# Full-height contraction for the product that adds the row maxima in an attention kernel

## The chip, the cores and the metric

The kernel runs on one core of one Trainium2 chip. The metric is device time in microseconds (us) of one launch, from the runs shown below. TensorE (PE in the profile, PEld for its weight loads) multiplies, VectorE (DVE), ScalarE (ACT) and GpSimd (POOL) do the elementwise work, and SyncE (SP) issues most DMAs. Every engine takes its own instructions in their written order and waits on semaphores.

## What is computed

The input x is 16 batches of 512 tokens of 256 channels, in float32. Four layers follow one another, each on a layer norm of x and added back to x: a gated delta net (a recurrence over the tokens, 16 heads), a mixture of experts (16 experts, 4 chosen for a token, and one shared), causal softmax attention (16 heads of 16 channels, with RMS norm and rotary embedding of queries and keys), and the mixture again. Only the third layer is touched by the change:

```
attn = einsum('bhqd,bhkd->bhqk', q, k) / sqrt(16)
attn = softmax(attn + causal, axis=-1)        # causal: -inf above the diagonal
out  = einsum('bhqk,bhkd->bhqd', attn, v) @ Wo
```

A softmax needs the largest score of each query subtracted ahead of the exponential. The kernel does it on TensorE, while the scores are still being summed in PSUM.

## The kernel before

The first half of the span (up to about 2970 us) is the recurrence, a chain of small VectorE steps, with the first mixture beside it. The second half is attention and the second mixture of all 16 batches. `stages()` writes out one list of named stages in Python, by generators that are stepped in turn with rates and costs; each engine then goes through this list and emits its own part of each stage. So the order on every engine is fixed, and interleaves the attention of a batch b, the end of the first mixture (batches 12 to 15, during the attention of batch 0), and the second mixture of earlier batches.

Attention of a batch: project (b_qk, b_v), normalize and rotate, split queries and keys into bfloat16 parts (s_...), turn them (s_turn), so that qT and kT hold 128 rows for each head (8 parts of 16 channels). Then come four groups of four heads. For a group, `largest(hg)` writes the scores with the queries on the partitions (m_dot, lines 1009 and 1011) and VectorE takes their row maxima, negated (m_max, L1367). The maxima are split into three bfloat16 parts (m_part), turned (m_turn, L1020) and copied by ScalarE into the tile mT: 12 rows (3 parts of 4 heads) by 512 queries (m_out, L1686). There are two mT tiles, one in the tile `region` and one in `w_attn`, which the profile names so.

`weigh(hg)` then makes the scores again, with the keys on the partitions, 16 times for a group (4 blocks of 128 keys by 4 heads; the width is 512, 384, 256 or 128 queries). This is w_dot, and it has three products into one PSUM bank: the scores (L1028, 128 rows of contraction), the negated maxima (L1030, 12 rows: a column of the selection matrix sel4 repeated over 128 columns, against the 12 rows of mT), and the causal mask on the diagonal block (L1032, 128 rows, 128 columns). ScalarE takes the exponential (w_exp, L1692) into one of eight buffers P, and w_pv (L1045) multiplies by the values, four heads side by side in 32 columns each. There are 16 x 4 x 16 = 1024 w_dots and 1024 m_dots. `largest(hg)` and `weigh(hg - 1)` are stepped in turn, so m_dot and w_dot alternate for three of the four weigh groups, and the last weigh group of a batch runs without m_dots.

PSUM banks come from the list `misc`: three banks until the first mixture is done, seven after that. m_max or w_exp gives the bank back.

In the second mixture, the tokens of a group of two or four batches are scattered to the rows of their experts in DRAM: x_row (ScalarE, L1721) makes a tile of 128 tokens and x_move (GpSimd, L1847) sends it with four indirect DMAs, for 8 or 16 tiles in a row. ScalarE waits in x_row until the move of two tiles before has landed.

GpSimd prepares the constants of attention once, in second_setup (L1820 to L1830): it counts the semaphore bset up to 7, and the engines that use a constant wait for its number. The lines around the change:

Of the kernel before, what the change touches and what calls it, by code (L numbers as in the profile page):

```python
# [9 lines left out]
BF = mybir.dt.bfloat16  # L10
# [4 lines left out]
NB, SEQ, D, H, HD = 16, 512, 256, 16, 16  # L15
# [703 lines left out]
def build(nc, T, out):  # L719
# [6 lines left out]
    psum = nc.alloc_psum_tensor("psum", [128, 8, 512], FP)  # L726
# [44 lines left out]
    def inshared(at, shape):  # L771
        return within(shared[:, at:at + math.prod(shape)], shape)
# [16 lines left out]
    lowerE, thr, tcol, upper32 = (inshared(2112, [NE, NE]), inshared(2368, [NE]), inshared(2384, [1]),  # L789
                                  inshared(2400, [128]))  # L790
    upper, onesb = shared[:, 2528:2592].bitcast(BF), shared[:, 2592:2656].bitcast(BF)
    sel4, sel432 = shared[0:12, 2916:2918].bitcast(BF), inshared(2920, [4])
    cosT, sinT = inshared(2924, [NQ, HD]), inshared(2988, [NQ, HD])
    qT, kT = partb(0, [16, 512]), partb(4096, [16, 512])
    vb = part(8192, [NQ, 16, 32])
# [55 lines left out]
    s = Sems(nc)  # L851
# [15 lines left out]
    def tensor():  # L867
# [4 lines left out]
        for name, *u in order:  # L872
# [149 lines left out]
            elif name == "w_dot":  # L1022
# [4 lines left out]
                pe.wait_ge(s[mf[0]], mf[1])  # L1027
                e.matmul(psum[:, mi, 0:n], kT[:, h, keys], qT[:, h, kt * 128:SEQ], start=True, stop=False,  # L1028
                         skip_group_check=True)
                e.matmul(psum[:, mi, 0:n], sel4[:, a:a + 1].broadcast_to([12, 128]), mT[k % 2][0:12, kt * 128:SEQ],  # L1030
                         start=False, stop=False, skip_group_check=True)
                o = e.matmul(psum[:, mi, 0:128], maskb[:, :], identb[:, :], start=False, stop=True,  # L1032
                             skip_group_check=True)
# [494 lines left out]
    def scalar():  # L1528
        ac = Eng(nc.scalar)
        e = nc.scalar  # L1530
        for name, *u in order:
# [98 lines left out]
            elif name == "f_up":  # L1630
                h, c, x, xi, xt, ti, gi, gf, si, sf = u
                ac.wait_ge(s["fup"], 34 * h + 17 * c + x + 1)
                ac.wait_ge(s[sf[0]], sf[1])
                if h >= 12:
                    o = e.activation(sil[si][:, :], psum[:, gi, 0:256], ACT.Tanh, scale=0.5)
                else:
                    o = e.activation(sil[si][:, :], psum[:, gi, 0:256], ACT.Silu)  # L1637
                o.then_inc(s["fs"], 1)
            elif name == "second_setup":
                ac.wait_ge(s["oadd"], 64)  # L1640

            elif name == "b_qk_out":
                i, mi, ai, af = u
                ac.wait_ge(s["qkm"], i + 1)
                ac.wait_ge(s["lo"], max(i - 3, 0))
                e.activation(qkr[i % 4], bank_of(mi), ACT.Copy).then_inc(s["qkc"], 1)
                ac.wait_ge(s[af[0]], af[1])
                e.activation(ra[ai], bank_of(mi), ACT.Square).then_inc(s["qks"], 1)
            elif name == "b_v_out":
                i, mi, ai = u  # L1650
                ac.wait_ge(s["vm"], i + 1)
                ac.wait_ge(s["pv"], 64 * (i // 4))
                ac.wait_ge(s["bset"], 7)
                e.activation(vb[:, i % 4, :, 0:16], psum[:, mi, 0:D].rearrange("p (h e) -> p h e", e=16),
                             ACT.Copy).then_inc(s["ve"], 1)
            elif name == "b_rms":
                b, = u
                ac.wait_ge(s["rm1"], b + 1)
                e.activation(rm, rm, ACT.Sqrt).then_inc(s["rm2"], 1)
            elif name == "s_hi":  # L1660
                i, ci, cf = u
                hh, cm = heads(qkr[i % 4]), comb3[ci]
                ac.wait_ge(s["spr"], 4 * i + 4)
                ac.wait_ge(s[cf[0]], cf[1])
                ac.wait_ge(s["pv"], 64 * (i // 4))
                e.activation(cm[:, 0:16, 0:3, :], bc(hh[:, 0:16, :], 2, 3), ACT.Copy)
                e.activation(cm[:, 16:32, 0:8:3, :], bc(hh[:, 16:32, :], 2, 3), ACT.Copy).then_inc(s["sph"], 1)
            elif name == "s_mid":
                i, ci = u
                hh, cm = heads(qkr[i % 4]), comb3[ci]  # L1670
                ac.wait_ge(s["r1"], 2 * i + 1)
                e.activation(cm[:, 16:32, 1:8:3, :], bc(hh[:, 16:32, :], 2, 3), ACT.Copy).then_inc(s["ma"], 1)
            elif name == "s_out":
                i, n, t, mi = u
                if n % 2:
                    j = slice(i % 4 * 128, i % 4 * 128 + 128)
                    ac.wait_ge(s["spt"], t)
                    ac.wait_ge(s["pv"], 64 * (i // 4))
                    e.activation((qT if n < 2 else kT)[:, 8:16, j],
                                 bank_of(mi).bitcast(BF).rearrange("p (h t) -> p h t", h=8),  # L1680
                                 ACT.Copy).then_inc(s["eva"], 1)
            elif name == "m_out":
                k, mi = u
                ac.wait_ge(s["pt"], k + 1)
                ac.wait_ge(s["ws"], 16 * max(k - 1, 0))
                e.activation(mT[k % 2][0:12, :], bank_of(mi).bitcast(BF)[0:12, 0:512], ACT.Copy).then_inc(s["mt"], 1)  # L1686
            elif name == "w_exp":
                k, kt, a, mi = u
                w, n = 16 * k + 4 * kt + a, SEQ - kt * 128
                ac.wait_ge(s["ws"], w + 1)  # L1690
                ac.wait_ge(s["pv"], max(w - 7, 0))
                e.activation(P[w % 8][:, 0:n], psum[:, mi, 0:n], ACT.Exp, scale=HD ** -0.5).then_inc(s["we"], 1)  # L1692
            elif name == "w_out":
                k, = u
                ac.wait_ge(s["pv"], 16 * k + 16)
                ac.wait_ge(s["pr"], k // 4 * 4)
                e.activation(oT[:, k % 4, :], psum[:, 6, :], ACT.Copy).then_inc(s["otr"], 1)
            elif name == "c_copy":
                i, mi, ci, cf = u
                ac.wait_ge(s["pt2"], i + 1)  # L1700
                ac.wait_ge(s[cf[0]], cf[1])
                e.activation(otc[ci][:, :, :], psum[:, mi, 0:256].rearrange("p (k t) -> p k t", k=2),
                             ACT.Copy).then_inc(s["poc"], 1)

            elif name == "g_score":
                b, mi, rf = u
                ac.wait_ge(s["glg"], b + 1)
                ac.wait_ge(s[rf[0]], rf[1])
                e.activation(r_sc, logits(bank_of(mi)), ACT.Tanh, scale=0.5).then_inc(s["gth"], 1)
            elif name == "g_act":  # L1710
                z, mi, si, sf = u
                ac.wait_ge(s["gu"], z + 1)
                ac.wait_ge(s[sf[0]], sf[1])
                e.activation(sil[si][:, :], psum[:, mi, 0:256], ACT.Tanh, scale=0.5).then_inc(s["gs"], 1)
            elif name == "x_row":
                g, J = u
                b, j = J // 4, J - ROWS0[g]
                ac.wait_ge(s["rv"], RV0[g] + 15 + 4 * GROUPS[g])
                if J >= 2:
                    ac.wait_ge(s[f"move{J % 2}"], 64 * (J // 2))  # L1720
                e.activation(srow[J % 2], x1[(b + 4) % 5][:, J % 4, :], ACT.Identity, bias=stq[:, j, 1:2],  # L1721
                             scale=stq[:, j, 0:1]).then_inc(s["row"], 1)
            elif name == "t_turned":
                I, mi = u
                ac.wait_ge(s["xT"], I + 1)
                ac.wait_ge(s["f1"], max(I - 1, 0))
                e.activation(xgT[I % 2], psum[:, mi, 0:256].rearrange("p (k t) -> p k t", k=2),  # L1727
                             ACT.Copy).then_inc(s["xe"], 1)
            elif name == "t_gate":
                I, mi, si, sf, hi, hf = u  # L1730
                ac.wait_ge(s["f1"], I + 1)
                ac.wait_ge(s[sf[0]], sf[1])
                e.activation(sil[si][:, 0:128], psum[:, mi, 0:128], ACT.Tanh, scale=0.5).then_inc(s["t1"], 1)  # L1733
            elif name == "t_hturned":
                I, mi = u
                ac.wait_ge(s["th"], I + 1)
                ac.wait_ge(s["f2"], max(I - 1, 0))
                e.activation(hT[I % 2], psum[:, mi, 0:128], ACT.Copy).then_inc(s["he"], 1)
            elif name == "t_out":
                g, I, mi = u  # L1740
                ac.wait_ge(s["f2"], I + 1)
                ac.wait_ge(s[f"yr{I % 2}"], 16 * (I // 2))
                e.activation(yrow[I % 2], psum[:, mi, 0:D], ACT.Copy).then_inc(s["yo"], 1)

    def gpsimd():
        po = Eng(nc.gpsimd)
        e = nc.gpsimd
        for name, *u in order:
# [71 lines left out]
            elif name == "second_setup":  # L1820
                po.wait_ge(s["oadd"], 64)
                po.wait_ge(s["d_b"], 176)
                e.tensor_copy(upper, upper32).then_inc(s["bset"], 1)
                e.tensor_copy(sel4, sel432[0:12, :]).then_inc(s["bset"], 1)
                e.memset(onesb, 1.0).then_inc(s["bset"], 1)
                e.tensor_tensor(cw, bc(cosT[:, :, :], 2, 2), bc(nw, 1, NQ), ALU.mult).then_inc(s["bset"], 1)
                e.tensor_tensor(sw, bc(sinT[:, :, :], 2, 2), bc(nws, 1, NQ), ALU.mult).then_inc(s["bset"], 1)
                e.memset(vb, 0.0).then_inc(s["bset"], 1)
                po.wait_ge(s["bset"], 6)
                e.memset(vb[:, :, :, 16:17], 1.0).then_inc(s["bset"], 1)  # L1830
            elif name == "g_score":
                b, mi, rf = u
                po.wait_ge(s[rf[0]], rf[1])
# [182 lines left out]
```

## Time and profile before

| | us |
|---|---|
| median of 3 runs | 5931.54 (5925.28 to 5931.58) |
| the profiled execution | 5932.07 |
| its span, first to last instruction | 5930.8 |
| PE busy | 4571.4 (77%) |
| DVE busy | 4165.5 (70%) |
| ACT busy | 1978.3 (33%) |
| POOL busy | 873.5 (15%) |
| mean granted TensorE clock | 0.883 of full speed |

"Busy" is an average over stages with different limits, so the table does not say what bounds the kernel. Matmuls overlap in the engine: the duration of one in the profile includes its way through the array, and what one costs on a busy TensorE is the distance from its start to the start of the next one. The chain of waits follows the execution back from its last instruction, and gives each engine and line the time for which it alone held up the end.

### The profile page before, as it was taken

Reading aid. Unit: us, or ns where it says so; the run is one execution under the profiler, and the core shown is the slowest. Engines: PE = TensorE matmul, PEld = TensorE weight load, DVE = VectorE, ACT = ScalarE, POOL = GpSimd, SP = SyncE. Lnnn points to the kernel's source line nnn. Section 1 sums busy time; section 2 is a strip of 40 time slices with the busy share of each in tenths; the row PEclk is TensorE's granted clock in tenths of the full one; section 3 lists DMA queues with packets and bytes.
Section 4 is the critical chain, followed back from the end, with each engine's and each line's share of the span. In section 5 each row is a group of like instructions: output and inputs, shape, how many; then the busy total and the mean of one; then the engine's idle time right before and its main releaser. Section 6 shows DMA issues by size and latency. Waiting matters only on the chain.

```text
span 5930.8 us, 70668 instructions
## 1 busy us (share of the span) xinstructions
PE 4571.4 (77%) x23962; PEld 3026.4 (51%) x23962; DVE 4165.5 (70%) x9356; ACT 1978.3 (33%) x4665; POOL 873.5 (15%) x1157
## 2 busy tenths in 40 slices
PE   6321188977988768877899879977999788978875
PEld 3110155655656556656667545543555455555553
DVE  1999999999999999994544555564555566555523
ACT  3111022212222121101322455553556455545442
POOL 2011011101010010001000020024000422023434
PEclk8655589998999989998999989987999799988987
DMA  1210000000000000000000011112111222122445
GB/s 73 112 41 5 2 10 11 11 4 15 10 12 4 9 6 8 8 4 27 11 4 8 8 44 43 44 56 71 43 45 48 85 76 86 46 74 71 140 149 155
DMA packets 192498, 249.28 MB, mean 42 GB/s; under 512 B 25744, under 2 KB 169744, under 8 KB 191888
## 3 DMA queue, kind: packets, MB, share of 16 engines
q1 hardware_dynamic: 167568, 177.63, 9.3%
q0 software_dynamic: 24576, 67.14, 3.6%
q8 instruction: 196, 3.21, 0.2%
q14 instruction: 158, 1.29, 0.1%
HBM read 120.94 MB, written 123.73 MB: 41 GB/s over the span
## 4 chain that ended last, share of the span: by engine, by line
PE 44%; DVE 36%; issue 9%; POOL 4%; ACT 4%; DMA 2%; SPq 0%; DVEq 0%; ACTq 0%; POOLq 0%
PE psum L956 7%; DVE rec L1200 4%; DVE rec L1213 4%; DVE rec L1202 4%; DVE skb L1205 4%; DVE rec L1216 4%; PE psum L973 4%; PE psum L1030 4%; PE psum L1131 3%; POOL xbuck L1847 3%; PE psum L987 3%; PE psum L1045 3%; PE psum L1032 2%; DVE region L1208 2%; PE psum L1028 2%
## 5 line engine op out<-in xcount | busy, mean ns | idle before, releaser
L956 PE MATMUL psum<-xnT,w_w13T 128*128 128x256 f32 x4352 | 1077.4, 392 | 0.0
L956 PEld LDWEIGHTS psum<-xnT,w_w13T 128*128 128x128 f32 x4352 | 845.3, 197 | 148.2 <-issue 27.7
L973 PE MATMUL psum<-w_w2T,hid 128*128 128x256 f32 x2176 | 622.2, 409 | 229.8 <-DVE hid L1292 216.7
L1367 DVE TENSOR_REDUCE region<-psum 128x1 f32<-128x384 f32 (+3 forms) x704 | 440.4, 639 | 415.8 <-PE psum L1011 409.0
L1637 ACT ACTIVATE sil<-psum 128x256 f32<-128x256 f32 x408 | 156.7, 384 | 1381.4 <-PE psum L956 1361.3
L1154 DVE SCALAR_TENSOR_TENSOR sil<-sil,psum 128x128 f32<-128x128 f32 (+1 forms) x504 | 165.7, 329 | 606.7 <-ACT sil L1733 388.5
L1692 ACT ACTIVATE region<-psum 128x512 f32<-128x512 f32 (+3 forms) x1024 | 437.5, 437 | 382.4 <-PE psum L1032 357.1
L973 PEld LDWEIGHTS psum<-w_w2T,hid 128*128 128x128 f32 x2176 | 380.0, 193 | 352.5 <-DVE hid L1292 271.7
L1131 PE MATMUL psum<-w_w13T,region 128*128 x1344 | 382.4, 410 | 16.7 <-ACT region L1727 11.5
L1213 DVE TENSOR_TENSOR rec<-ub,region 128x512 f32<-128x512 f32 x512 | 377.7, 738 | 8.0
L882 PE MATMUL psum<-w_ident,xn 128*128 128x128 f32 x512 | 96.1, 319 | 367.8 <-ACT xn L1542 364.5
L1216 DVE TENSOR_TENSOR rec<-rec 128x512 f32<-128x512 f32 x512 | 351.9, 687 | 10.4 <-ACT sil L1637 2.5
L1200 DVE TENSOR_TENSOR rec<-rec,region 128x512 f32<-128x512 f32 x512 | 351.9, 687 | 8.1
L1202 DVE TENSOR_TENSOR rec<-rec,region 128x512 f32<-128x512 f32 x508 | 351.9, 693 | 0.0
L1205 DVE TENSOR_REDUCE skb<-rec 128x32 f32<-128x512 f32 x512 | 346.9, 678 | 0.1
L1208 DVE TENSOR_REDUCE region<-rec 128x32 f32<-128x512 f32 x508 | 342.6, 674 | 0.0
L1761 POOL TENSOR_SCALAR small<-small 128x4 f32<-128x4 f32 (+1 forms) x80 | 31.3, 391 | 2096.2 <-DVE small L1167 2094.9
L1028 PE MATMUL psum<-region 128*128 128x512 bf16 (+3 forms) x1024 | 325.8, 318 | 12.0 <-ACT region L1686 4.4
L1009 PE MATMUL psum<-region 128*128 128x128 bf16 (+3 forms) x1024 | 282.5, 317 | 60.3 <-ACT region L1692 48.9
L1857 POOL DMA_INDIRECT region<-ybuck,rec x256 | 252.5, 986 | 438.9 <-DVE region L1525 249.6
L1144 PE MATMUL psum<-w_w2T,region 128*128 x672 | 231.0, 428 | 70.9 <-issue 56.3
L1847 POOL DMA_INDIRECT xbuck<-region,rec x256 | 248.1, 969 | 232.3 <-ACT region L1721 156.7
(226 smaller groups left out, 8344.8 us busy)
## 6 DMA issues: line engine op xcount, KB each, us to landing
ybuck<-region SPq DMA_DIRECT2D x336, 128.0 KB
region<-xbuck SPq DMA_DIRECT2D x202, 128.0 KB, 2.2
xbuck<-x SPq DMA_DIRECT2D x40, 512.0 KB, 5.3
scale<-xbuck SPq DMA_DIRECT2D x134, 128.0 KB, 2.2
x_scratch<-x SPq DMA_DIRECT2D x16, 512.0 KB, 3.2
x_scratch<-region SPq DMA_DIRECT2D x32, 256.0 KB, 2.2
region<-x_scratch SPq DMA_DIRECT2D x64, 128.0 KB, 2.8
out<-region SPq DMA_DIRECT2D x64, 128.0 KB
```

Of the source, the lines that this page charges most:

```text
L956: o = e.matmul(psum[:, gi, m * 256:m * 256 + 256], w13T[:, x, k, m * 128:(m + 1) * 128], xnT[xi][:, k, cols], start=(k == 0), stop=(k == 1 ...
L973: o = e.matmul(psum[:, yi, j * D:(j + 1) * D], hid[hi][:, j * 128:(j + 1) * 128], w2T[:, x, :], start=(x == 0 and j == 0), stop=(x == NX - ...
L1028: e.matmul(psum[:, mi, 0:n], kT[:, h, keys], qT[:, h, kt * 128:SEQ], start=True, stop=False, skip_group_check=True)
L1131: o = e.matmul(psum[:, mi, 0:256], xgT[I % 2][:, k, :], w13T[:, bass.ds(expert[I], 1), k, :].rearrange("p a b -> p (a b)"), start=(k == 0) ...
L1200: e.tensor_tensor(tk[:, :, :, :], S[:, :, :, :], ktt, ALU.mult).then_inc(s["scan"], 1)
L1202: e.tensor_tensor(tq[:, :, :, :], S[:, :, :, :], bc(kq[:, :, t - 1, 16:32], 2, 16), ALU.mult).then_inc(s["scan"], 1)
L1205: e.tensor_reduce(skb[:, :, :], tk[:, :, :, :], AX.X, ALU.add).then_inc(s["scan"], 1)
L1208: e.tensor_reduce(vo[:, :, t - 1, :], tq[:, :, :, :], AX.X, ALU.add).then_inc(s["scan"], 1)
L1213: e.tensor_tensor(tk[:, :, :, :], bc(ub[:, :, :], 3, 16), ktt, ALU.mult).then_inc(s["scan"], 1)
L1216: e.tensor_tensor(S[:, :, :, :], S[:, :, :, :], tk[:, :, :, :], ALU.add).then_inc(s["scan"], 1)
L1367: e.tensor_reduce(mx[:, qt, h0:h0 + nh], psum[:, mi, 0:nh * n].rearrange("p (a k) -> p a k", a=nh), AX.X, ALU.max, negate=True).then_inc(s ...
L1692: e.activation(P[w % 8][:, 0:n], psum[:, mi, 0:n], ACT.Exp, scale=HD ** -0.5).then_inc(s["we"], 1)
```

## The change

The product L1030 contracts over all 128 partitions. For that, sel4 is made for 128 partitions in place of 12 (the rows from 12 on are zero in the constant that is loaded already), and both mT tiles are set to zero once in second_setup, so that the 116 rows below the 12 that m_out writes are zero. m_out waits for the two memsets. The products, their number, their widths and their order stay as they were.

```diff
-    sel4, sel432 = shared[0:12, 2916:2918].bitcast(BF), inshared(2920, [4])
+    sel4, sel432 = shared[:, 2916:2918].bitcast(BF), inshared(2920, [4])
...
-                e.matmul(psum[:, mi, 0:n], sel4[:, a:a + 1].broadcast_to([12, 128]), mT[k % 2][0:12, kt * 128:SEQ],
+                e.matmul(psum[:, mi, 0:n], sel4[:, a:a + 1].broadcast_to([128, 128]), mT[k % 2][:, kt * 128:SEQ],
                          start=False, stop=False, skip_group_check=True)
...
             elif name == "m_out":
                 k, mi = u
                 ac.wait_ge(s["pt"], k + 1)
+                ac.wait_ge(s["bset"], 9)
                 ac.wait_ge(s["ws"], 16 * max(k - 1, 0))
...
-                e.tensor_copy(sel4, sel432[0:12, :]).then_inc(s["bset"], 1)
+                e.tensor_copy(sel4, sel432).then_inc(s["bset"], 1)
...
                 po.wait_ge(s["bset"], 6)
                 e.memset(vb[:, :, :, 16:17], 1.0).then_inc(s["bset"], 1)
+                e.memset(mT[0], 0.0).then_inc(s["bset"], 1)
+                e.memset(mT[1], 0.0).then_inc(s["bset"], 1)
```

## Rows read from the trace of the kernel before

**Rows 1.** The page: the span in 40 slices of 148.3 us, in tenths.

```profile
PE   6321188977988768877899879977999788978875
DVE  1999999999999999994544555564555566555523
```

**Rows 2.** Busy time by stretch of the weigh stage; columns stand in the first row.

```profile
core 0: us, PE busy (x) PEld busy (x) DVE busy (x) ACT busy (x) POOL busy (x), PEclk, DMA share, GB/s
3530.00:4039.00 509.00, 436.94 (x2930) 275.50 (x2928) 311.49 (x766) 274.43 (x622) 49.49 (x80) 0.92 0.14 44
4039.00:4118.00 79.00, 59.58 (x300) 22.47 (x300) 30.40 (x85) 27.46 (x65) 58.51 (x63) 0.64 0.29 103
4118.00:4672.00 554.00, 492.25 (x3308) 316.55 (x3307) 319.92 (x824) 315.17 (x761) 31.01 (x64) 0.95 0.15 47
...
4750.00:5304.00 554.00, 473.15 (x3205) 302.32 (x3204) 346.63 (x880) 304.50 (x731) 90.19 (x122) 0.95 0.22 68
```

**Rows 3.** Chain of waits from 2979 to 5528 us, shares by line.

```profile
by line: PE psum L1030 8.3%; issue 7.1%; PE psum L1045 5.9%; PE psum L987 5.8%; PE psum L1032 5.6%; POOL xbuck L1847 5.6%; PE psum L1028 5.4%; PE psum L956 5.0%; PE psum L1131 4.8%; PE psum L1009 4.6%; PE psum L973 2.8%; PE psum L997 2.5%; 
```

**Rows 4.** Timeline of an m_dot: start us, duration us, engine, line, operation, tiles, shapes.

```profile
3034.70 0.38 PE L1009 MATMUL psum<-region 128*128 128x512 bf16 x1
3034.70 0.10 PEld L1011 LDWEIGHTS psum<-maskbb,identb 128*128 128x128 bf16 x1
3034.92 0.22 PE L1011 MATMUL psum<-maskbb,identb 128*128 128x128 bf16 x1
```

**Rows 5.** Timeline of a w_dot of width 512, and the next one's start.

```profile
4551.00 0.39 PE L1028 MATMUL psum<-region 128*128 128x512 bf16 x1
4551.31 0.09 PEld L1030 LDWEIGHTS psum<-w_attn 12*128 12x128 bf16 x1 [0.23 <-issue]
4551.32 0.39 PE L1030 MATMUL psum<-w_attn 12*128 12x512 bf16 x1
4551.63 0.10 PEld L1032 LDWEIGHTS psum<-identb,maskbb 128*128 128x128 bf16 x1 [0.23 <-issue]
4551.64 0.23 PE L1032 MATMUL psum<-identb,maskbb 128*128 128x128 bf16 x1
...
4551.70 0.38 PE L1028 MATMUL psum<-region 128*128 128x512 bf16 x1
```

**Rows 6.** Timeline of a w_dot of width 128, matmuls only.

```profile
4561.46 0.22 PE L1028 MATMUL psum<-region 128*128 128x128 bf16 x1
...
4561.61 0.23 PE L1030 MATMUL psum<-w_attn 12*128 12x128 bf16 x1
...
4561.77 0.23 PE L1032 MATMUL psum<-identb,maskbb 128*128 128x128 bf16 x1
...
4561.84 0.22 PE L1028 MATMUL psum<-region 128*128 128x128 bf16 x1
```

**Rows 7.** Timeline of a w_dot's last product and the w_pv behind it.

```profile
4560.13 0.23 PE L1032 MATMUL psum<-identb,maskbb 128*128 128x128 bf16 x1
4560.29 0.16 PEld L1045 LDWEIGHTS psum<-region 128*32 128x32 f32 x8
```

**Rows 8.** The page's costliest groups: w_dot's first product.

```profile
L1028 PE MATMUL psum<-region 128*128 128x512 bf16 (+3 forms) x1024 | 325.8, 318 | 12.0 <-ACT region L1686 4.4
```

**Rows 9.** ScalarE's groups by shape: the exponentials of width 512 and 128.

```profile
L1692 ACT ACTIVATE region<-psum 128x512 f32<-128x512 f32 x256 | 150.9, 595 | 108.6 <-PE psum L1032 104.5
...
L1692 ACT ACTIVATE region<-psum 128x128 f32<-128x128 f32 x256 | 69.5, 278 | 66.0 <-PE psum L1032 52.4
```

**Rows 10.** Busy time in a batch's last weigh group, columns as in Rows 2.

```profile
4551.00:4563.00 12.00, 12.00 (x79) 4.79 (x77) 0.00 (x0) 8.39 (x22) 0.00 (x0) 1.00 0.07 23
```

**Rows 11.** GpSimd's groups from 4039 to 4118 us.

```profile
L1847 POOL DMA_INDIRECT xbuck<-region,rec x59 | 57.1, 968 | 49.4 <-ACT region L1721 32.0 <-issue 17.4
```

**Rows 12.** GpSimd's groups by shape, second_setup.

```profile
L1828 POOL MEMSET region<- 128x2048 f32 x1 | 1.8, 1796 | 0.0
...
L1823 POOL CAST w_attn<-w_attn 128x128 bf16<-128x128 f32 x1 | 0.3, 291 | 11.1 <-DMA w_attn<-in_sel 11.1
```

## The prediction

> **What bounds the kernel now.** I read the slices first: up to slice 20 VectorE is full, and from slice 21 (about 2970 us) TensorE is at 7 to 9 tenths with VectorE at 4 to 6 [rows 1]. All w_dots lie in that second half. By stretches TensorE is busy for 436.94 of 509 us, 492.25 of 554 and 473.15 of 554, and the other engines for at most 346.63 of 554; the exceptions are the stretches in which GpSimd scatters, such as 4039 to 4118 us, where GpSimd is busy for 58.51 of 79 us and TensorE's clock is at 0.64 [rows 2]. A busy share does not prove a bound, so the chain comes next: from 2979 to 5528 us (2549 us) the chain has L1030 as its largest line with 8.3%, that is 212 us, then L1032 with 5.6% and L1028 with 5.4% [rows 3]. w_dot is the largest thing that holds up the end there.
>
> Then the timeline, for what one product costs: the distance from start to start. In an m_dot both products have 128 rows. The weight load of L1011 starts together with the matmul of L1009 (3034.70), so it is hidden, and L1011 starts 0.22 us after L1009, which is 512 columns at 2.4 GHz [rows 4]. In a w_dot of the same width, L1028 starts at 4551.00 but the 12-row load of L1030 starts only at 4551.31 and its matmul at 4551.32: 0.32 us for the same 512 columns. The load of L1032 again starts only at 4551.63, just ahead of its matmul: 0.32 us. After L1032, 128 columns, the next product is 0.06 us later [rows 5]. At width 128 the three distances are 0.15, 0.16 and 0.07 us [rows 6], where the same 128 columns cost 0.06 after L1032 in rows 5. So each of the two passages, from 128 rows to 12 and from 12 back to 128, costs about 0.10 us, at either width: a fixed price that depends on the change of height, not on how long the product is.
>
> **The change part by part.**
>
> 1. *The passages go.* With 128 rows everywhere in the w_dot, its loads should start behind the running matmul as in an m_dot. Width 512: from 0.32 + 0.32 + 0.06 = 0.70 us [rows 5] to 0.22 + 0.22 + 0.06 = 0.50 [rows 4]. Width 128: from 0.38 [rows 6] to 3 x 0.06 = 0.18. So 0.20 us for a w_dot at both ends of the widths, and I take it for all four. There are 1024 [rows 8]: 205 us of TensorE's time. The columns that stream stay the same, since a product's time goes with its columns: the 12-row product of 512 columns lasts 0.39 us and the 128-row one 0.38 to 0.39 [rows 5].
>
> [...]
>
> 2. *What of it is on the path.* In the chain a piece of L1030 runs from the end of L1028 to its own end. If every w_dot were on the chain, its pieces would come to 1024 times the mean of the distances at both ends, (0.32 + 0.15)/2 = 0.235 us [rows 5, 6], so 241 us. It has 212 [rows 3]: 88%. The rest lies in the stretches where GpSimd scatters and TensorE waits [rows 2, 11]. 0.88 x 205 = 180 us.
>
> 3. *What is late next.* In the last weigh group of each batch no m_dot lies between the w_dots. From 4551 to 4563 us TensorE is busy for all of 12.00 us and ScalarE for 8.39 [rows 10]. TensorE's part would shrink by 16 x 0.20 = 3.2 us to 8.8, and in its first four w_dots the exponential (0.595 us) would be slower than the w_dot (0.50), as it would be at width 128 (0.278 against 0.18) [rows 9]. Seven banks and eight P buffers hide part of this, but w_pv waits for the exponentials, so I take back 0.8 us for each of 16 batches: 13 us. This is my estimate, from nothing (8.8 is still over 8.39) to 3.2 us (all of it, 51 us). In the other weigh groups an m_dot lies beside each w_dot and costs at least 0.22 + 0.06 us at width 512, so 0.78 us a pair against 0.595 us of ScalarE: TensorE stays the limit. For new waits elsewhere, where VectorE's or GpSimd's answer is now just in time, I take another 2 us or so, which is a choice; the range holds more.
>
> 4. *The weight load of L1030 with 128 rows.* sel4 is one column repeated 128 times, and no full-height load of that kind is in the trace. A dense full-height load lasts 0.10 us and the repeated 12-row one 0.09 [rows 4, 5]. Lower bound: hidden, no cost. Upper bound: it is never hidden, and the first passage stays, 0.10 x 1024 x 0.88 = 90 us less gain (a rival below). I take it as hidden, by the nearest row, L1011's load [rows 4].
>
> 5. *The memsets, the copy of sel4 and the new wait.* A memset of 128x2048 float32 lasts 1.796 us [rows 12]; each mT tile has an eighth of these bytes, so two cost between 0.4 us (by size) and 3.6 us (if size did not matter), once, on GpSimd, which is mostly idle then. The copy of 128x128 to bfloat16 took 0.291 us [rows 12], so that of 128x4 lies between nothing and that. The wait stands ahead of each m_out on ScalarE, and every later exponential and copy of ScalarE is queued behind it, for which TensorE would wait. But the GpSimd work of second_setup stands in its order well ahead of the first m_out, and once bset is 9 the wait costs nothing. If this cover were gone, the price would be the 3.6 us once. I take 0.
>
> Sum against the profiled execution, 5932.07 us (span 5930.8 and 1.3 around it): 5932 - 180 + 13 + 2 = 5767. That execution is within 0.6 us of the median 5931.54, so nothing has to be shifted. I say 5765 us, 2.8% faster. Its own range is 5735 (all 205 us but a few on the path, ScalarE never late) to 5805 (on the path only 70% of it, 143, and 16 of it given back to ScalarE).
>
> **The rivals.**
>
> *One passage stays.* The repeated column at full height is read in another way and its load is not hidden, or the passage costs because the stationary operand changes its kind. For it: no row shows such a load. Against: the passage into w_pv, from 128 columns to 32 at full height, with another type and no repetition, also costs 0.16 us in place of 0.06 [rows 7], so it is the change of shape that costs. Time: 5932 - 90 + 5 = about 5845.
>
> *The gain is given back.* TensorE comes early to waits on ScalarE and GpSimd. For it: ScalarE's exponentials are slower than a shortened w_dot; in the scatter stretch ScalarE's x_row makes GpSimd wait 32.0 us and GpSimd's issues take 57.1 of 79 us [rows 11], and the chain has 5.6%, 143 us, of those issues in all [rows 3]. Against: the stretches between them have a TensorE share of 85 to 89% with ScalarE at 54 to 57% [rows 2]. If half of the 180 us is lost, 5842; with two thirds kept, 5812.
>
> *No change.* Full-height loads are hidden behind matmuls of the same height only because in m_dot something else frees them, and in w_dot the loads stay exposed. Then each passage stays 0.10 us and the time is 5932. Against: L1028 behind L1032 is 0.06 us away [rows 5], within the w_dot chain itself. [...]
>
> *Slower.* The clock. TensorE stood at 0.64 where it waited for GpSimd, against 0.92 to 0.95 in the long stretches [rows 2]. If, with w_dots shorter, its idle pieces grow so that it is granted 1.2 GHz for more of the time, matmuls that now take 1402 us (436.94 + 492.25 + 473.15) get longer. At a mean clock of 0.79 in these three (halfway down to the 0.64), in place of about 0.94, that is 1402 x (0.94/0.79 - 1) = 266 us: 5765 + 266 = about 6030. It decides from a clock of 0.94 x 1402/(1402 + 167) = 0.84 down. Against: rows 10 has the clock at 1.00, and what is removed is time in which the array streamed nothing, so its work gets denser.
>
> **How the numbers follow.** Forecast 0.74, one passage stays 0.09, given back 0.09, no change 0.05, slower 0.03. A change of over 0.2% (12 us) can be told from none. Faster: 0.74 + 0.09 + 0.09 = 0.92, same 0.05, slower 0.03. The range of 5720 to 5850 takes in the forecast, most of the case of one passage and of the case given back, and leaves out no change, slower and a little at both ends: about 0.8.
>
> **What would show each step.** In the profile after: L1030's loads, now of 128 rows, start with the matmul ahead of them, and the distances at width 512 are 0.22, 0.22 and 0.06 (step 1 and 4). The chain's share of L1030 falls from 212 us to about 0.14 us x 1024 x 0.88 = 126 us (step 2). The last weigh group of a batch takes 9 to 10 us in place of 12, with ScalarE nearly full (step 3). The first 2970 us stay as they are (step 5). The forecast is wrong if the distances stay at 0.32, if TensorE's idle time in the second half grows by more than 60 us, or if the mean clock of the long stretches falls under 0.9.

## The result and the profile after

The changed kernel takes 5755.05 us (median of 4 runs, 5748.21 to 5761.49), the kernel before on the same chip 5928.41 us. The ratio is 0.9713, with a 95% interval from 0.9691 to 0.9736: 173 us or 2.9% faster. The prediction was 5765 us. The profiled execution of the changed kernel has a span of 5746.9 us, 183.9 under that of before.

The slices of the page after, of 143.7 us each. The first eighteen differ from those before by one tenth at most [rows 1]. From 2979 us to the end TensorE is busy for 82% of less time, where it was 84%:

```profile
PE   6322078977889768887899978886889688977875
DVE  1999999999999999998354565665566566655533
PEclk8655589999999989999899988997999899988887
```

The timeline of a w_dot of width 512 in a last weigh group, which answers to [rows 5]:

```profile
4427.43 0.38 PE L1028 MATMUL psum<-region 128*128 128x512 bf16 x1
4427.44 0.10 PEld L1030 LDWEIGHTS psum<-w_attn 128*128 128x128 bf16 x1
4427.65 0.38 PE L1030 MATMUL psum<-w_attn 128*128 128x512 bf16 x1
4427.65 0.10 PEld L1032 LDWEIGHTS psum<-identb,maskbb 128*128 128x128 bf16 x1
4427.86 0.22 PE L1032 MATMUL psum<-identb,maskbb 128*128 128x128 bf16 x1
4427.87 0.10 PEld L1028 LDWEIGHTS psum<-region 128*128 128x128 bf16 x1
4427.92 0.38 PE L1028 MATMUL psum<-region 128*128 128x512 bf16 x1
```

Each weight load now starts with the matmul ahead of it, and the distances from start to start are 0.22, 0.21 and 0.06 us in place of 0.32, 0.32 and 0.06. The load of the repeated column at full height is hidden as a dense one is. At width 128, answering to [rows 6]:

```profile
4434.16 0.22 PE L1032 MATMUL psum<-identb,maskbb 128*128 128x128 bf16 x1
...
4434.22 0.22 PE L1028 MATMUL psum<-region 128*128 128x128 bf16 x1
...
4434.27 0.22 PE L1030 MATMUL psum<-w_attn 128*128 128x128 bf16 x1
...
4434.33 0.22 PE L1032 MATMUL psum<-identb,maskbb 128*128 128x128 bf16 x1
```

Three times 0.05 to 0.06 us. The durations, 0.38 us at width 512 and 0.22 at 128, are 0.16 us longer than these distances at both widths; by that much a product overlaps with the next. Over all 1024 w_dots the medians are 216, 163, 109 and 56 ns for both passages at the four widths, where they were 312 and 317, 258 and 264, 205 and 211, 152 and 157 ns; the product after L1032 comes 56 ns later in place of 66. That is 96 + 101 + 10 = 207 ns a w_dot, the same at all widths, and 212 us in all. These are the medians; 967 of the 1024 w_dots after ran wholly at a granted clock of 1.00. There, 384 columns more take 216 - 56 = 160 ns more, which is 2.4 columns a ns; that is what the runs show of the 2.4 GHz in the prediction.

The chain of waits from 2979 to 5349 us, which answers to [rows 3]:

```profile
by line: issue 8.5%; POOL xbuck L1850 7.5%; PE psum L987 6.2%; PE psum L1045 5.7%; PE psum L956 5.2%; PE psum L1131 5.1%; PE psum L1028 5.0%; PE psum L1030 4.4%; PE psum L1009 4.2%; PE psum L973 2.9%; PE psum L1144 2.7%; PE psum L997 2.6%; 
```

L1030 has 4.4% of 2370 us, 104 us in place of 212, and L1032 has left the list. GpSimd's scatter (L1850, L1847 before) has grown from 143 to 178 us: it takes over part of what TensorE gave up. GpSimd works no longer than before: the 64 issues of the scatter in batch 10 take 83.0 us before and 82.9 after, and in the first three weigh groups of that batch their share of the chain goes from 45.8% to 59.1%.

Busy time by stretch after, columns as in [rows 2]; the first is a long stretch, the second a batch's last weigh group [rows 10], the third the first three weigh groups of batch 10, under GpSimd's scattering:

```profile
4097.00:4500.00 403.00, 365.86 (x2757) 260.37 (x2757) 253.08 (x654) 253.49 (x634) 13.90 (x39) 0.97 0.16 51
```

```profile
4426.60:4435.00 8.40, 8.40 (x73) 4.83 (x75) 0.00 (x0) 6.77 (x20) 0.00 (x0) 1.00 0.10 32
```

```profile
4520.90:4609.20 88.30, 50.39 (x400) 28.10 (x398) 36.86 (x106) 32.41 (x83) 59.50 (x64) 0.85 0.28 100
```

And the last of these in the kernel before, found in the same way (from the group's first exponential to the last):

```profile
4649.10:4740.10 91.00, 69.73 (x388) 30.00 (x389) 37.38 (x105) 34.03 (x83) 61.22 (x66) 0.66 0.29 100
```

The long stretch keeps TensorE at 91% with the clock at 0.97. The last weigh group is still TensorE's, for all of its 8.40 us. Under the scatter TensorE is busy for 50.39 us in place of 69.73, and the stretch is only 2.7 us shorter: GpSimd's issues of L1850 set its length.

### The profile page after: what moved, and what is told of

Read it like the earlier page. It is cut to its first block, busy times and chain, and to the rows that moved or that the text cites. A ratio compares the mean times of both kernels' runs of the same rounds, so it can differ in the third digit from the quotient of the medians.

```text
span 5746.9 us, 70671 instructions
## 1 busy us (share of the span) xinstructions
PE 4334.5 (75%) x23962; PEld 3031.9 (53%) x23962; DVE 4153.2 (72%) x9356; ACT 1945.3 (34%) x4665; POOL 872.5 (15%) x1159
## 4 chain that ended last, share of the span: by engine, by line
PE 41%; DVE 38%; issue 10%; POOL 5%; ACT 4%; DMA 2%; SPq 0%; DVEq 0%; ACTq 0%; POOLq 0%
PE psum L956 7%; DVE rec L1200 5%; DVE rec L1213 4%; DVE rec L1202 4%; DVE skb L1205 4%; DVE rec L1216 4%; PE psum L973 4%; POOL xbuck L1850 3%; PE psum L1131 3%; PE psum L987 3%; DVE region L1208 2%; PE psum L1045 2%; PE psum L894 2%; PE psum L1028 2%; PE psum L1030 2%
## 5 line engine op out<-in xcount | busy, mean ns | idle before, releaser
L956 PE MATMUL psum<-xnT,w_w13T 128*128 128x256 f32 x4352 | 1068.1, 389 | 0.0
L956 PEld LDWEIGHTS psum<-xnT,w_w13T 128*128 128x128 f32 x4352 | 840.0, 195 | 146.1 <-issue 27.4
L973 PE MATMUL psum<-w_w2T,hid 128*128 128x256 f32 x2176 | 620.9, 409 | 234.3 <-DVE hid L1292 221.3
L973 PEld LDWEIGHTS psum<-w_w2T,hid 128*128 128x128 f32 x2176 | 378.9, 192 | 357.1 <-DVE hid L1292 276.8
L1693 ACT ACTIVATE region<-psum 128x512 f32<-128x512 f32 (+3 forms) x1024 | 407.8, 439 | 215.6 <-PE psum L1032 205.5
L1028 PE MATMUL psum<-region 128*128 128x512 bf16 (+3 forms) x1024 | 310.7, 312 | 28.9 <-DVE region L1367 9.3
L1850 POOL DMA_INDIRECT xbuck<-region,rec x256 | 247.7, 967 | 229.2 <-ACT region L1722 153.9
```

The costliest lines, as they stand in the source:

```text
L956: o = e.matmul(psum[:, gi, m * 256:m * 256 + 256], w13T[:, x, k, m * 128:(m + 1) * 128], xnT[xi][:, k, cols], start=(k == 0), stop=(k == 1 ...
L973: o = e.matmul(psum[:, yi, j * D:(j + 1) * D], hid[hi][:, j * 128:(j + 1) * 128], w2T[:, x, :], start=(x == 0 and j == 0), stop=(x == NX - ...
L1850: e.indirect_dma_start(xbuck[g % 2], bass.IndirectOffsetOnAxis(ap=posu[g % 2][:, J - ROWS0[g], k:k + 1], axis=0), srow[J % 2], None).then_ ...
```

## The experiments

The question is what makes a w_dot with 12 rows dear. Theory A: the price belongs to the passage between a product of few rows and one of full height, about 0.10 us each way as at 12 rows (0.32 us in place of 0.22 at width 512) [rows 4, 5], and from some height under 128 on there is none. That 96 rows would count as full height (5755 us), and 32 and 64 as few (the time of before), like the 48 rows in the mixture below, was the author's guess, which no run had shown. Rivals: any change in the number of rows costs, so that 96, 64 and 32 all take the time of before (theory B); the price goes with the missing rows (theory C); or short weight loads can never be hidden. The first four kernels ran on one chip, where the kernel before takes 5928.61 us (median of 25), the next four on another, where it takes 6041.28 (median of 13), and the last four on a third, where it takes 5927.88 (median of 7). Ratios are taken to the kernel before on the same chip.

**Height of the product.** The edit, in the changed kernel, with 96, 64 or 32 for N:

```diff
-  e.matmul(..., sel4[:, a:a + 1].broadcast_to([128, 128]), mT[k % 2][:, kt * 128:SEQ],
+  e.matmul(..., sel4[0:N, a:a + 1].broadcast_to([N, 128]), mT[k % 2][0:N, kt * 128:SEQ],
```

> The changed kernel, but the product of L1030 takes 96 rows of sel4 and mT in place of 128; the other two products of a w_dot keep 128. [...] Theory B (any change in the number of rows costs, whatever the mode): 0.31 us twice, and about 5928 us. Theory C (the price goes with the rows that are missing): 32 of 116 missing rows, so about 5755 + 0.28 x 173 = 5803 us.

> The same with 64 rows. [...] Theory C: 64 of 116 missing rows, about 5755 + 0.55 x 173 = 5850 us.

> The same with 32 rows. Theories A and B: 5928 us, distances of 0.31 us. Theory C: about 5755 + 0.83 x 173 = 5898 us. A rival D, that it is the odd number of 12 rows that costs, and a whole strip of 32 would not: 5755 us.

Measured: 96 rows 5755.93 us, ratio 0.9701 (0.9682 to 0.9721); 64 rows 5914.40, 0.9974 (0.9964 to 0.9984); 32 rows 5916.41, 0.9984 (0.9971 to 0.9997). The timeline at width 512 with 96 rows:

```profile
4438.37 0.38 PE L1028 MATMUL psum<-region 128*128 128x512 bf16 x1
4438.37 0.10 PEld L1030 LDWEIGHTS psum<-w_attn 96*128 96x128 bf16 x1
4438.58 0.38 PE L1030 MATMUL psum<-w_attn 96*128 96x512 bf16 x1
...
4438.80 0.22 PE L1032 MATMUL psum<-identb,maskbb 128*128 128x128 bf16 x1
```

And with 64 rows:

```profile
4531.40 0.38 PE L1028 MATMUL psum<-region 128*128 128x512 bf16 x1
4531.71 0.09 PEld L1030 LDWEIGHTS psum<-w_attn 64*128 64x128 bf16 x1 [0.26 <-issue]
4531.72 0.39 PE L1030 MATMUL psum<-w_attn 64*128 64x512 bf16 x1
...
4532.03 0.23 PE L1032 MATMUL psum<-identb,maskbb 128*128 128x128 bf16 x1
```

96 rows beside 128 cost next to nothing (0.21 and 0.22 us, by the medians 6 ns more a w_dot than 128), though the number of rows changes; 64 cost the full 0.32 and 0.31, and 32 the same (medians at width 512 of 312 and 319 ns with 64 rows, 312 and 317 with 32). There is nothing between, so a price by missing rows is out, and so is any change of rows. Of the three theories only A fits. What the chip tells 96 from 64 by is not seen in a row, only that the step lies between them, and whether a change between two short heights, 32 and 64, costs was not tried.

The kernels with 96 and 64 rows differ in nothing but this number, and ran on one chip: 158 us lie between them, and 160 between 96 and 32. That is the best measure here of what the passages alone are worth, and it is less than the 173 us of the whole change. The 64 and 32 rows came out 0.26% and 0.16% under the kernel before (14 and 12 us), though their distances are those of before. Most of that is the granted clock in two places of the traces. Batch 1's first three weigh groups take 49.9 us in the kernel before, with a clock of 0.86, and 45.4 and 45.3 with 64 and 32 rows, at 0.97. Batch 3's last weigh group takes 15.0 us before, at 0.61, and 10.6 in both others, at 1.00:

```profile
3656.20:3671.50 15.30, 15.30 (x69) 5.01 (x72) 0.57 (x2) 7.53 (x19) 0.00 (x0) 0.61 0.03 10
```

TensorE is busy throughout; the clock records of the traces hold only 0.50 and 1.00, so it was granted 0.50 for most of the group. The changed kernel has 0.96 and 1.00 in these two places. So some 9 us of the 173 came with the clock and not with the products; why more was granted was not tried. In batch 1 the traces of rows12 and split12, also with 12 rows, have the 0.86 as well, so it need not be chance.

**Passage or load.** The 12-row product of the kernel before in two halves, with the second's load at the same height:

```diff
-                e.matmul(psum[:, mi, 0:n], sel4[...], mT[k % 2][0:12, kt * 128:SEQ], ...)
+                for c in (0, n // 2):
+                    e.matmul(psum[:, mi, c:c + n // 2], sel4[...],
+                             mT[k % 2][0:12, kt * 128 + c:kt * 128 + c + n // 2], ...)
```

> The kernel before with the 12-row product made in two halves of the columns, one behind the other: the same columns in all, one more weight load and one more 12-row product in each of 1024 w_dots, and still two passages. If the price belongs to the passage between heights, the second half starts n/2 columns after the first (0.109 us at width 512), nothing is added but the load behind short halves, and the time is 5928 us with up to 20 us more. If the price belongs to each 12-row weight load (a short load can never hide behind a running matmul), each w_dot has 0.10 us more, 0.10 x 1024 x 0.88 = 90 us: 6018 us.

Measured: 5936.96 us, ratio 1.0015 (1.0001 to 1.0028), 8 us more. The timeline at width 512 (two loads and two products are merged into one row each):

```profile
4544.75 0.38 PE L1028 MATMUL psum<-region 128*128 128x512 bf16 x1
4545.06 0.11 PEld L1031 LDWEIGHTS psum<-w_attn 12*128 12x128 bf16 x2 [0.27 <-issue]
4545.06 0.39 PE L1031 MATMUL psum<-w_attn 12*128 12x256 bf16 x2
4545.38 0.10 PEld L1034 LDWEIGHTS psum<-identb,maskbb 128*128 128x128 bf16 x1 [0.21 <-issue]
4545.38 0.23 PE L1034 MATMUL psum<-identb,maskbb 128*128 128x128 bf16 x1
```

From L1028 to L1034 it is 0.63 us, as with one 12-row product: two of them, one behind the other, pay the passage once in and once out. What the merged rows hide, the same trace has one by one: the second 12-row load starts 0.01 us after the first half's matmul, and the second half's matmul 0.12 us after it (median at width 512, where 256 more columns take 216 - 109 = 107 ns more in the trace of the changed kernel). A 12-row load hides behind a 12-row product, so the rival that short loads can never be hidden is out: it wanted 6018 us.

**What else the change adds.** The changed kernel with 12 rows in the product:

```diff
+  e.matmul(..., sel4[0:12, a:a + 1].broadcast_to([12, 128]), mT[k % 2][0:12, kt * 128:SEQ],
```

> The changed kernel with everything it adds (sel4 and mT at 128 rows, the two memsets, m_out's wait for them), but the product of L1030 still takes 12 rows. If those additions cost nothing: the time of the kernel before, 5928 us. If they cost what step 5 gave as its upper end, up to 4 us more. If they had a hidden share in the gain (for instance by where things start), less than 5928 us.

Measured: 6049.40 us, ratio 1.0009 (0.9994 to 1.0024). No difference can be told from none, so neither cost nor gain comes from what else the change adds. In the changed kernel the two memsets took 0.544 and 0.525 us, from 2731.4 us on, and the first m_out comes 240 us later.

**The last weigh groups and the others.** A quarter of the w_dots, and the complement:

```diff
+                tall = 128 if k % 4 == 3 else 12      # last128;  k % 4 < 3: first128
+                e.matmul(psum[:, mi, 0:n], sel4[0:tall, a:a + 1].broadcast_to([tall, 128]),
+                         mT[k % 2][0:tall, kt * 128:SEQ], ...)
```

> 128 rows only in the last weigh group of each batch (a quarter of the w_dots, those with no m_dot between them), 12 rows in the others. If ScalarE holds nothing back there, 16 x 0.207 = 3.3 us for each of 16 batches, 53 us: 5876 us. If ScalarE takes back 0.8 us for a batch, as step 3 has it, 40 us: 5889 us.

> The complement: 128 rows in the first three weigh groups, 12 in the last. 768 w_dots of 0.207 us are 159 us; these groups hold all that GpSimd's scattering hides, so the whole gain of 173 us less that of the last groups (40 to 53 us) is left: 120 to 133 us, that is 5795 to 5808 us. If the two parts help or hinder one another, the gains of the two kernels do not add up to 173 us.

Measured: last128 5968.82 us, ratio 0.9877 (0.9855 to 0.9898), 72 us; first128 5926.78 us, 0.9820 (0.9794 to 0.9846), 115 us. The 72 us are more than either expectation, also as a share (1.2% against 0.9%), and the 115 us fewer than expected (1.8% against 2.0 to 2.2%). The two gains sum up to 3.0%, and the whole change has 2.9 to 3.0% on other chips (0.9713 and, with 96 rows, 0.9701), so within some 0.3% they neither help nor hinder one another; the whole change did not run on this chip. On this chip the scatter stretches are longer (105 to 107 us for the first three weigh groups of batches 6, 10 and 14, where the other has 88 to 91), as GpSimd's 64 issues take 93 to 96 us there in place of 83, which hides more of first128.

A good part of the rest of last128's 72 us is the granted clock. Its trace can be laid beside that of rows12, which has 12 rows in all w_dots on the same chip and took 81 us longer. Here are batch 6's last weigh groups, rows12 first:

```profile
4158.40:4174.80 16.40, 16.40 (x65) 4.13 (x68) 0.00 (x0) 7.47 (x17) 0.00 (x0) 0.50 0.01 2
```

```profile
4119.70:4126.90 7.20, 7.20 (x69) 3.87 (x70) 0.00 (x0) 6.19 (x17) 0.00 (x0) 1.00 0.32 93
```

The change accounts for about 3 us of these 9, the clock for the rest. Batches 5 and 12 have the like (12.5 us at 0.64 and 15.1 at 0.60, in the kernel before on the first chip 9.9 and 10.9 at 1.00), and batch 1's first three groups, in which last128 changes nothing, get 4.6 us shorter with a clock of 0.97 for 0.86. Together that is some 17 of the 28 us that this pair has beyond 53. Whether the higher clock is owed to the change or to chance one trace each cannot tell.

For the changed kernel, from the first exponential of a last weigh group to its last, all 16 together take 192.3 us before and 140.9 after. That is 51.4 us, of which batch 3's group with the low clock has 7.5. Thirteen of the others get 2.9 to 3.2 us shorter each, and the last two, at a clock of 0.88 after, 2.0 and 1.9. From the first exponential to the last lie 15 w_dots, 15 x 0.207 = 3.1, so ScalarE takes back almost nothing.

**Where the missing part went.** Half of the scattering left out, under the kernel before and under the changed one (the counts that engines wait for are halved with it; half of the second mixture's rows are then missing, and the work on them is the same):

```diff
-                for k in range(4):
+                for k in range(2):
                     e.indirect_dma_start(
                         xbuck[g % 2], ...)
```

> The kernel before, with two of the four indirect DMAs of each x_move left out (half the rows of the second mixture are not scattered; all that is computed of them still runs). It is the base for half128. The chain has 143 us of these issues; half of them gone, and TensorE taking over as the limit, gives about 60 to 110 us less than the kernel before.

> The changed kernel with the same two DMAs left out. 1024 w_dots give back 0.207 us each, 212 us, but the span fell by 184 only, 175 of it between the first w_dot and the last. Theory A (the missing part is hidden under the scattering, where TensorE waits for GpSimd): with half the scattering the change is worth more than 175 us, about 190 to 205 us against half12. Rival (the missing part is lost to ScalarE's exponentials and to VectorE, all over the weigh stage): the difference stays at about 175 us.

Measured: half12 5829.73 us, ratio 0.9841 (0.9818 to 0.9863); half128 5640.03 us, 0.9516 (0.9494 to 0.9539). The difference is 190 us, 16 more than with the whole scatter, but the spread of the runs leaves the 190 open by about 11 us either way and the 173 by about 13, so the totals alone do not decide. The stretches below run from the first to the last exponential of a batch's first three weigh groups; the columns are the stretch, its length, ScalarE's busy time in the exponentials (48 of them), the clock, DMA share and GB/s. Batch 10 with half of the scatter, under the kernel before:

```profile
4611.00:4675.10 64.10, 20.03 (x48) 0.87 0.24 83
```

And under the changed one; the second row is batch 9, with no scatter:

```profile
4479.10:4537.50 58.40, 18.57 (x48) 0.85 0.25 89
4344.50:4383.30 38.80, 19.95 (x48) 1.00 0.12 35
```

With half of the scatter this stretch gets 5.7 us shorter by the change, with the whole of it 2.7 (91.0 to 88.3). Batch 9 gets 8.9 us shorter in the full kernels (from 4502.0 to 4549.7 before, from 4386.3 to 4425.1 after), of 47 x 0.207 = 9.7. Over batches 6, 10 and 14 the first three weigh groups took 88, 91 and 88 us before and 88, 88 and 88 after: 3 us of the 30 that their 144 w_dots could give. These 27 us are most of the 37 between 212 and the 175 by which the time from the first w_dot to the last fell; batch 2's groups, beside 32 scatter issues, miss another 5. With half of the scatter the same three batches give 12 us and batch 2's 8, so 12 us more come out from under the scatter: theory A of this experiment is shown by its stretches. The total of 190 is no measure of it, since batch 1's first three groups alone, with no scatter beside them, have 24.5 us (60.4 to 35.9): half12's trace stands at a clock of 0.67 there, where the kernel before has 0.86 and 49.9 us.

**The same for the mixture.** The product L963 repeats a column of 48 rows between products of 128:

```diff
-    self32, sel = sb("w_sel", [48, NE]), sb("selb", [48, NE], BF)
+    self32, sel = sb("w_sel", [128, NE]), sb("selb", [128, NE], BF)
-    combT = [sb(f"combT{i}", [48, 512], BF) for i in range(2)]
+    combT = [sb(f"combT{i}", [128, 512], BF) for i in range(2)]
-                    o = e.matmul(psum[:, 3, 0:256], sel[:, x:x + 1].broadcast_to([48, 128]), combT[ti][:, cols],
+                    o = e.matmul(psum[:, 3, 0:256], sel[:, x:x + 1].broadcast_to([128, 128]), combT[ti][:, cols],
...
+                e.memset(combT[0][:, :], 0.0).then_inc(s["set"], 1)
+                e.memset(combT[1][:, :], 0.0).then_inc(s["set"], 1)
```

Not shown are the 80 zero rows in the constant behind sel, and in the copy into combT its 48 rows and its wait for the memsets.

> The changed kernel, and beside it the product that spreads the mixture's weights (L963, 48 rows between products of 128) gets 128 rows too: combT is zeroed once, sel has 80 zero rows more. By theory A each of 512 products gives back two passages, 0.20 us. 384 of them lie beside VectorE's recurrence in the first half and bring nothing; 128 lie from 2980 to 3310 us, where TensorE is full: 26 us, so 5755 - 26 = 5729 us. If VectorE or the latency between the engines is the limit there, it stays at 5755 us.

> The changed kernel once more, unaltered, to stand beside comb128b on one chip: a ratio to the kernel before of 0.971.

> comb128 once more, on the chip of the changed kernel: by theory A, with 128 of its 512 products on the path, 26 us less than the changed kernel, a ratio of 0.967. If all of the difference between 0.9653 and 0.9713 is the product's, 0.965.

Measured: comb128 5829.67 us, ratio 0.9653 (0.9632 to 0.9675); again 5754.12 us, 0.9713 (0.9691 to 0.9735); comb128b 5719.64 us, 0.9645 (0.9626 to 0.9664). So 34 us less than the changed kernel on one chip, and the fastest version here. Its timeline:

```profile
3008.55 1.03 PE L956 MATMUL psum<-xnT,w_w13T 128*128 128x256 f32 x4
3009.41 0.27 PE L963 MATMUL psum<-combT,selb 128*128 128x256 bf16 x1
3009.52 0.33 PE L1028 MATMUL psum<-region 128*128 128x384 bf16 x1
```

L963 comes 216 ns after the last L956 (312 ns before), and the next product 110 ns after it (211), by the medians. From the first product of batch 12's mixture to the last of batch 15's, the traces have 524.6 us, in the changed kernel's repeated run 546.3: 22 us, with 128 of the L963 products in it (26 expected). Another 10 us are gone before that, where none was expected; by which wait they come was not tried. The expectation had misplaced these 128 products: the first of them comes at 2758 us, and only 73 come behind the first w_dot. VectorE's recurrence ends at 2694 us, and from 2670 to 2979 us VectorE is busy for 51% of the time and TensorE for 84%, so the last 300 us of the first half are not VectorE's. What the two memsets and the wait add was not run by itself.

## Why the prediction was right, step by step

The prediction read VectorE as full up to slice 20. The slices before have it full for 18 of them, to 2670 us, and at 4 and 5 tenths in the next two [rows 1]. The forecast does not hang on this, as all w_dots lie behind 2979 us; the expectation of comb128 does.

1. *The passages go*: right, 0.207 us a w_dot where 0.20 stood, at all four widths. That the passage from few rows costs, and not every change in their number, is shown by 12, 32 and 64 rows (312 ns in and 317 to 319 out, at width 512) beside 96 (216 and 220) and 128 (216 and 216); what the engine does in the 0.10 us is not seen in a row. That a full-height load hides behind a full-height product is shown too: the 128-row load of 4427.44 starts 0.01 us after the 128-row matmul of 4427.43.
2. *On the path*: the chain gave 88%, 180 us. From the first w_dot to the last the traces fell by 175 us, 83% of 212. The kind was right (the scatter stretches hide the rest), and the stretches of half128 show it; the share was too high because a chain counts what holds up the end now. In batch 10's scatter stretch L1030 still had 5.5% of the chain before, and has 0.6% after: when its pieces got shorter, GpSimd's grew (143 to 178 us in all) beside them. So L1030 has 104 us of the chain after, where the prediction expected 126.
3. *What is late next*: the term that was mis-sized. 13 us were taken back for the last weigh groups, 0.8 us for a batch; the quiet groups show 0.2 us at most. ScalarE's pace was read from the duration of one exponential, 0.595 us [rows 9]. Queued, they overlap. The timeline after:

```profile
4427.15 1.58 ACT L1693 ACTIVATE region<-psum 128x512 f32<-128x512 f32 x3 [0.28 <-PE psum L1032]
```

The three start 0.493 and 0.488 us apart, which is the pace of the w_dots (0.216 + 0.216 + 0.056 = 0.488), and only the last one's end adds its full 0.595. Where two exponentials of width 512 do stand in a queue, the second starts 0.477 us after the first (median of 72 pairs), and at width 128 it is 0.157; the kernel before has the same 0.477 in 34 pairs, so it could have been read there. The shortened w_dot takes 0.488 and 0.168. ScalarE is a little faster at both, and TensorE stays busy for all of 8.40 us with ScalarE at 6.77, where 9 to 10 us with ScalarE nearly full were expected. The 2 us for new waits elsewhere can't be told apart.
4. *The load of the repeated column*: right, hidden; "one passage stays" is refuted.
5. *Memsets and wait*: right, nothing (rows12), 1.07 us of GpSimd's time with 240 us of cover.

That 173 us came so near to the 167 forecast is partly luck. The gain of a w_dot was 7 us too small in all, the share on the path too high (88% of 212 would be 187, and 175 came), and the 15 us taken back for steps 3 and beyond were hardly there; these cancel. Some 9 us of the 175 came with the clock in batches 1 and 3 besides. Without them the share is 78%, and the kernels with 96 and 64 rows put the gain at 158. The two profiled spans differ by 184: 175 between the first and the last w_dot, 3 before and 5 behind them, where the change does nothing. The changed kernel's repeated run has 181 between its first w_dot and its last, so such a figure is good to some 6 us.

"Given back" happened in the scatter stretches, 27 us in three of them and 5 in batch 2's. TensorE's idle time from 2979 us on grew by 46 us (461 to 506), under the 60 that would have shown the forecast wrong. "Slower" did not happen: the clock of the long stretches is 0.94 to 0.97, and in the scatter stretch of batch 10 it rose from 0.66 to 0.85, though TensorE's busy share there fell from 77% (69.73 of 91.00 us) to 57% (50.39 of 88.30). What the traces show of the 1.2 GHz of that rival is the granted clock of 0.50, at which 512 columns take 427 ns in the changed kernel in place of 216, 1.2 columns a ns.

## What to carry to other kernels

Where a product of few rows stands between products of full height, read the distances from start to start and not the durations: a load that starts just ahead of its matmul, at each passage between 12, 48 or 64 rows and 128, was 0.10 us here, and zero rows gave it back. Between 96 rows and 128 there was nothing to give back (6 ns a w_dot). Zero padding cost nothing here (rows12, a ratio of 1.0009), where the padded rows are written once and never again. Read the pace of a queued engine from the distance between the starts of two queued instructions, and not from the duration of one (here 0.477 us against 0.595). Before a difference of some 10 us is given to a change, compare the granted clock of the same stage in both traces. And count what lies beside another engine's fixed work at nothing, even where the chain still gives it a share (here 5.5% for L1030 in batch 10's scatter stretch, which got 2.7 of 91.0 us shorter).

## What the runs showed that was not expected

The step lies between 64 and 96 rows, and short heights cost the same as one another: 12, 32, 48 and 64 rows all pay about 0.10 us in and 0.10 us out next to 128 (at width 512, 312 ns in place of 216 and 317 to 319 in place of 216; around L963 with 48 rows, 312 in place of 216 and 211 in place of 110). At the lower clock the passage costs more: 87 w_dots of the kernel before ran wholly at a granted clock of 0.50, with distances of 567 and 535 ns at width 512 (22 of them; such is that from 3325.80 us on) where the kernel after has 427 at that clock. That is 0.14 us in and 0.11 out, while the time of the columns itself doubled (216 to 427). Narrow products pay too: L1045, with 32 columns at full height, still comes 0.15 us after L1032 (128 columns wide; median of 185, where the next w_dot comes 0.056 us after it). The float32 type alone does not cost this: L956 and L973, in float32 with 128 columns, come 0.06 us after L1032 (medians of 7 and 9), so what is left is the width; no run changed it alone. In the scatter stretch of batch 10 the changed kernel's matmuls were busy for 50.39 us in place of 69.73, for the same products, 19 us less where 10 were removed. The clock of 0.85 in place of 0.66 fits the rest, and it bought nothing, since GpSimd set the end.
